# Three bias products of an attention item in row groups of their own, and all rounds of a four-layer cross-attention kernel written out

## The reference

```python
# layers 0, 2
q, k, v = rmsnorm(x, norm_w) @ wq, cond @ wk, cond @ wv     # 16 query heads, 4 key heads
out = x + (softmax(q k^T / sqrt(8)) v) @ wo
# layers 1, 3
col_bias = jnp.zeros((HW, T))                               # 128 tokens x 77 keys
col_bias = col_bias.at[:, token_indices_A].set((-SUPPRESS * (1.0 - mask_A))[:, None])
col_bias = col_bias.at[:, token_indices_B].set((-SUPPRESS * (1.0 - mask_B))[:, None])
logits = einsum('bhqd,bhkd->bhqk', q, k) * scale + col_bias
out = (softmax(logits) v) @ Wo + bo + x
```

## Time and profile before

| | |
|---|---|
| median of 3 runs | 1966.53 us |
| profiled execution | 1973.73 us, its span 1971.9 us |
| TensorE busy | 1882.1 us (95%) |
| VectorE, GpSimd, ScalarE busy | 1677.6 (85%), 1496.9 (76%), 1453.1 us (74%) |
| DMA, transposes and loads | 88.1% share of the 16 engines |
| bias products (L1266) | 384, three per MHA item of 128 |
| mean granted clock of TensorE | 0.969 |

### The profile page before, as it was taken

How to read it: one execution, slowest core, us unless ns; L and a number is a source line. 1 busy time by engine, 2 the same in 40 slices (tenths; PEclk the granted TensorE clock), 3 DMA queues, 4 the chain that set the end, 5 groups by cost and what they waited for, 6 DMA issues and landing times.

```text
span 1971.9 us, 76204 instructions
## 1 busy us (share of the span) xinstructions
PE 1882.1 (95%) x28656; PEld 1578.3 (80%) x28784; DVE 1677.6 (85%) x3516; ACT 1453.1 (74%) x2603; POOL 1496.9 (76%) x1830
## 2 busy tenths in 40 slices
PE   5599999999999999999999999999999999999996
PEld 5478888888788887888788887888878888888884
DVE  7588888898788987888888988889878898888883
ACT  4377777777777776777777777777767777777772
POOL 2478888788787877788777887878878888888872
PEclk7599999999999999999999999999999999999997
DMA  5279999999899998899979997999989999999985
GB/s 160 50 126 167 162 168 167 169 160 163 155 174 167 159 168 150 168 162 161 168 150 169 159 166 145 175 169 160 165 150 176 163 163 163 159 152 170 160 158 107
DMA packets 1164823, 310.79 MB, mean 158 GB/s; under 512 B 1139254, under 2 KB 1163132, under 8 KB 1164412
## 3 DMA queue, kind: packets, MB, share of 16 engines
q1 hardware_dynamic: 1164412, 305.43, 88.1%
HBM read 15.93 MB, written 4.19 MB: 10 GB/s over the span
## 4 chain that ended last, share of the span: by engine, by line
PE 81%; DMA 5%; issue 3%; DVE 3%; SPq 3%; POOL 2%; ACT 2%; ACTq 0%; DVEq 0%
PE ring L1135 46%; PE sc L1268 9%; PE o_ps L1135 8%; DMA arena<-p_sm 5%; PE o_ps L1286 4%; PE ring L1337 4%; PE sc L1251 3%; PE sc L1266 2%; POOL arena L589 1%; PE ring L1206 1%; POOL p_sm L566 1%; ACT arena L627 1%; PE ring L1318 1%; PE ring L1334 1%; PE sc L1243 1%
## 5 line engine op out<-in xcount | busy, mean ns | idle before, releaser
L561 POOL TENSOR_TENSOR p_sg<-arena,p_sg 128x512 f16<-128x512 f32 (+1 forms) x256 | 347.4, 1357 | 216.1 <-ACT p_sg L627 216.1
L1135 PE MATMUL ring<-ctx_two,m_w 128*128 128x154 f16 x6144 | 447.1, 233 | 0.0
L1135 PEld LDWEIGHTS ring<-ctx_two,m_w 128*128 128x128 f16 x6144 | 433.7, 99 | 1.0 <-DVE o_tg L821 0.9
L1004 DVE TENSOR_TENSOR arena<-sc,row_max 128x616 f32<-128x616 f32 (+2 forms) x512 | 405.2, 792 | 4.5
L566 POOL TENSOR_TENSOR p_sm<-arena,p_sm 128x616 f16<-128x616 f32 x256 | 336.8, 1316 | 46.9 <-ACT p_sm L627 46.9
L1135 PE MATMUL ring<-wv_m,ctx_two 128*77 128x512 f16 x1536 | 365.5, 383 | 0.1
L627 ACT ACTIVATE arena<-ring 128x462 f16<-128x462 f32 (+1 forms) x384 | 196.3, 512 | 136.9 <-PE ring L1135 136.9
L589 POOL TENSOR_TENSOR arena<-arena 128x1024 f16<-128x1024 f32 x128 | 273.1, 2133 | 30.2 <-ACT arena L627 19.1
L1135 PEld LDWEIGHTS ring<-wv_m,ctx_two 128*77 128x77 f16 x1536 | 166.0, 117 | 149.9 <-DVE q_mix L825 46.1
L1001 DVE TENSOR_REDUCE row_max<-sc 128x6 f32<-128x462 f32 (+2 forms) x384 | 223.7, 582 | 55.6 <-PE sc L1268 55.5
L1268 PE MATMUL sc<-arena,x_s 128*128 128x512 f16 (+1 forms) x1152 | 262.5, 337 | 7.0
(11 more groups left out here) (160 smaller groups left out, 3529.9 us busy)
## 6 DMA issues: line engine op xcount, KB each, us to landing
ctx_nat<-in_ctx_dram SPq DMA_DIRECT2D x64, 77.0 KB
x_nat<-in_x_dram SPq DMA_DIRECT2D x64, 64.0 KB, 2.2
arena<-p_sg SPq DMA_TRANSPOSE x256, 4.2
arena<-p_sm SPq DMA_TRANSPOSE x256, 3.9
out_dram<-y_out SPq DMA_DIRECT2D x64, 64.0 KB, 2.0
arena<-in_L_xattn_Wk_dram SPq DMA_DIRECT2D x2, 1024.0 KB, 6.0
arena<-in_L_xattn_Wv_dram SPq DMA_DIRECT2D x2, 1024.0 KB, 6.7
arena<-arena SPq DMA_TRANSPOSE x128, 5.8
```

The costliest lines, as they stand in the source:

```text
L561: pool.tensor_tensor(p_sg[k][:, LO, 0:e - a], probs_flat[:, a:e], p_sg[k][:, HI, 0:e - a], ALU.subtract).then_inc(sems["pg_lo"], 1)
L1004: dve.tensor_tensor(shifted[:, hs, :], s_view[:, hs, :], row_max[:, hs].unsqueeze(2).to_broadcast([P, hs.stop - hs.start, S]), ALU.subtrac ...
L1135: ins = pe.matmul(out, a, b, start=(n == 0), stop=(n == len(passes) - 1))
```

## The change

All three bias products of an MHA item are issued together, ahead of the scores of chunk 0. Each takes its six rows from another group of 32 partitions: the product of bank b reads partitions 32b to 32b + 5 of `bias_l` and `bias_r`. For that the prologue copies the six rows to partitions 32 and 64, six more steps of VectorE. Since all three banks are opened at chunk 0, `scores_free` waits there for both halves of the shift, and no longer at chunks 1 and 2. And the loops over the rounds are gone on all five engines: rounds 1 to 7 are written out.

```diff
--- before.py
+++ after.py
@@ -487,11 +487,9 @@
 
             for n in range(-3, PAIRS):
                 pair(0, n)
-            with sp.Fori(1, NIT - 2) as it:
+            for it in range(1, NIT):
                 for n in range(PAIRS):
                     pair(it, n)
-            for n in range(2 * PAIRS):
-                pair(NIT - 2 + n // PAIRS, n % PAIRS)
             for n in range(TAIL):
                 pair(NIT, n)
             for st in range(STREAMS):
@@ -612,11 +610,9 @@
 
             for n in range(-3, PAIRS):
                 pair(0, n)
-            with pool.Fori(1, NIT - 1) as it:
+            for it in range(1, NIT):
                 for n in range(PAIRS):
                     pair(it, n)
-            for n in range(PAIRS):
-                pair(NIT - 1, n)
             for n in range(TAIL):
                 pair(NIT, n)
 
@@ -805,11 +801,9 @@
 
             for n in range(-3, PAIRS):
                 pair(0, n)
-            with act.Fori(1, NIT - 1) as it:
+            for it in range(1, NIT):
                 for n in range(PAIRS):
                     pair(it, n)
-            for n in range(PAIRS):
-                pair(NIT - 1, n)
             for n in range(TAIL):
                 pair(NIT, n)
 
@@ -919,6 +913,10 @@
                 step(dve.tensor_scalar(m[5], mask_p[:, 0, :], row_sel[:, 0:1], None, ALU.mult))
                 step(dve.scalar_tensor_tensor(out=m[6], in0=mask_p[:, 1, :], scalar=row_sel[:, 1:2], in1=m[5], op0=ALU.mult, op1=ALU.add))
                 step(dve.scalar_tensor_tensor(out=bias_l[0:6, :], in0=mask_p[:, 2, :], scalar=row_sel[:, 2:3], in1=m[6], op0=ALU.mult, op1=ALU.add))
+                for k in range(1, 3):
+                    step(dve.tensor_copy(bias_l[32 * k:32 * k + 6, :], bias_l[0:6, :]))
+                    for n in range(2):
+                        step(dve.tensor_copy(bias_r[n][32 * k:32 * k + 6, :, :], bias_r[n][0:6, :, :]))
 
             def split_gqa_weights():
 
@@ -1117,11 +1115,9 @@
 
             for n in range(-3, PAIRS):
                 pair(0, n)
-            with dve.Fori(1, NIT - 1) as it:
+            for it in range(1, NIT):
                 for n in range(PAIRS):
                     pair(it, n)
-            for n in range(PAIRS):
-                pair(NIT - 1, n)
             for n in range(TAIL):
                 pair(NIT, n)
 
@@ -1260,10 +1256,14 @@
                 lead = leader(m)
                 g = g_s[lead // 4 % 2][:, :, stream(m) % 2].rearrange("p a h s -> p a (h s)")
                 pe.wait_ge(sems["g_lo"], at("g_lo", it, lead, G_NEEDED[k]))
-                scores_free(it, m, min(k, 1) + 1)
-                ind = bias_r[w][:, :, :].rearrange("p h s -> p (h s)")
                 a, e = k * BANK, min(HS, (k + 1) * BANK)
-                pe.matmul(sc_flat[:, a:e], bias_l[:, :], ind[:, a:e], start=True, stop=False)
+                if k == 0:
+
+                    scores_free(it, m, 2)
+                    ind = bias_r[w][:, :, :].rearrange("p h s -> p (h s)")
+                    for b in range(3):
+                        c0, c1, rows = b * BANK, min(HS, (b + 1) * BANK), slice(32 * b, 32 * b + 6)
+                        pe.matmul(sc_flat[:, c0:c1], bias_l[rows, :], ind[rows, c0:c1], start=True, stop=False)
                 for x, y in ((HI, HI), (HI, LO), (LO, HI)):
                     ins = pe.matmul(sc_flat[:, a:e], x_s[st][:, x, :], g[:, y, a:e], start=False, stop=(x == LO))
                 ins.then_inc(sems["sm_raw"], 1)
@@ -1375,11 +1375,9 @@
 
             for n in range(-3, PAIRS):
                 pair(0, n)
-            with pe.Fori(1, NIT - 1) as it:
+            for it in range(1, NIT):
                 for n in range(PAIRS):
                     pair(it, n)
-            for n in range(PAIRS):
-                pair(NIT - 1, n)
             for n in range(TAIL):
                 pair(NIT, n)
 
@@ -1387,7 +1385,7 @@
 CONSTS = 19
 ARENA = 15180
 SMALL_LOADS = 20
-DVE_STEPS = 73
+DVE_STEPS = 79
 
 
 # ---- launch: one core; inputs and output as the reference has them ----
```

## The result

| | before | changed |
|---|---|---|
| median | 1965.45 us (4 runs) | 1952.12 us (4 runs, 1951.14 to 1953.31) |
| ratio | | 0.9932, 95% interval 0.9915 to 0.9949 |
| profiled execution, span | 1973.73, 1971.9 us | 1952.95, 1951.2 us |
| short pair, long pair | 13.93, 14.44 to 14.58 us | 14.18, 14.44 us |
| TensorE busy | 1882.1 us | 1871.1 us |

The kernel is 13 us faster, 0.7%. The forecast was 25 us (1941 us, in a range of 1926 to 1976). The two halves of the change pull in opposite directions, as the experiments will show: written-out rounds give about 30 us, grouped bias products take 16 back.

What follows compares the result with a forecast made beforehand. TensorE was taken as the main bound (81% of the chain). Loops -28.1, prologue +3.0, short pairs +12.0 and long pairs -12.3 sum to -25.4: 1948.3 us from the profiled execution, 1941 after the 7.2 to the median; range 1926 to 1976.

Steps and rivals of the forecast that it cites:

- Loops written out: At the jumps between the six loop rounds: writing them out removes the jumps and what follows them, -28.1 us.
- the aftermath: Behind each jump: pipeline refilled by VectorE, GpSimd and the transposes, counted within the 28.1 us.
- Prologue: Ahead of the rounds: six more VectorE steps, all on the path, +3.0 us (2.0 to 3.7).
- The group of three: Ahead of chunk 0's scores: three bias products run side by side in 0.24 us, or 0.52 if one waits for another.
- one after another: Rival, at the group: the three bias products run serially, 0.52 us, 36 us more, 1977 us; 5%.
- The wait at chunk 0: First bias load: 0.38 us late behind the second shift in short pairs, none in long; short pairs net +12.0 us.
- Chunk 2's 0.09 us lost to q_mix: Behind `values_m`: the 0.09 us saved at chunk 2 turns into a longer TensorE wait for q_mix.
- Going into and out of row groups: Around each item's bias group: changing from all rows to 32 and back costs 0, at the other end +50 us.
- the 30% rival: Around the bias products: the mode change empties the array, 0.16 or 0.26 us each, 192 times, 1972 or 1991 us; 30%.
- No new wait: Rival, at chunk 0: VectorE keeps up, 0.28 us an item is kept, -36 us, 1905 us; 4%.
- The jumps aren't the cost: Rival, at the loops: straight code stalls as often, only prologue and bias count, 1969 us; 6%.
- Transposes become the bound: Rival, in pairs that get shorter: transposes bound them, long pairs stay as they are, +12, 1953 us; 7%.

Runs made afterwards that it cites:

- e1: Changed kernel with the bias products of before, each ahead of its own chunk over all rows, without the prologue copies: 1935.79 us, 0.9843 of before.
- e6: Changed kernel, but all three grouped bias products take the same rows 0 to 5, without the prologue copies: 1986.02 us, 1.0098 of before.
- e7: e1 with each bias product, in its own place, restricted to rows 0 to 5: 2001.29 us, 1.0172 of before.
- e2: Kernel before, loops kept, with the three grouped bias products and the six prologue steps: 1983.42 us, 1.0077 of before.
- e10: e1 without the bias product of chunk 2: 1935.56 us, 0.9836 of before.
- e9: e7 with each bias product over rows 0 to 37, a group of 64 rows: 2002.99 us, 1.0190 of before.
- e8: Kernel before with its loops, each engine given a hint on its closing branch at the top of the body: 1944.99 us, 0.9884 of before.
- e11: e1 without the bias product of chunk 1: 1915.51 us, 0.9742 of before.
- e3: Changed kernel, but the three grouped bias products each run over all 128 rows, without the prologue copies: 1968.01 us, 1.0003 of before.

## Why the prediction came out as it did

**Loops written out: right, slightly too small.** -28.1 forecast; e1 gives -30.5 by the medians. A loop also held up pairs away from the jump, which my reference, the first loop round, contained. What the forecast called the aftermath, a pipeline refilled by VectorE, GpSimd and the transposes, is for the most part something else: TensorE at half its clock, about 12.7 of the 28.1 us. The size came from the windows and so was right without it.

**Prologue: right.** +3.0 against 2.5.

**The group of three: right.** The forecast had 0.24 us for the group and 36 us more if the products ran one after another. e6 against the changed kernel is 34 us, and 36 with the copies of the prologue, which e6 doesn't have. A group takes 0.32 us up to the first score, as long as the single product of e7: nothing is lost among the three. The rival "one after another" is out.

**The wait at chunk 0: right in place, kind, pairs and size.** Apart from three of the 67 waits only short pairs have it. Counted from the pair's start the load moved from 5.17 (e1) to 5.55 us, 0.37 us; 0.38 was forecast. Two small differences cancel here, which is luck: the load comes 0.11 us behind the shift instead of 0.05, but the shift itself ends 0.07 us earlier in the pair. In e2 the distance is 0.05 in the looped rounds, where a register instruction takes the other waits and sg_sub alone stands on the product, and 0.11 to 0.12 in its written-out rounds; their short pairs last 14.09 and 14.18 us. A short pair grew by 0.25 us instead of 0.19 because of the way out of the row group: the first score comes 0.46 us later than in e1, where 0.38 + 0.02 was due.

**Chunk 2's 0.09 us lost to q_mix: right**, shown by e10. The waits for q_mix are 53.9 us in the changed kernel against 43.1 in e1, 0.09 each.

**Going into and out of row groups: this is the step that failed.** The forecast took 0, from "the nearest row", and named what it didn't show. There the products change from one half of the partitions to the other, at the same height. Measured are about 0.10 us on the way in and 0.08 to 0.10 on the way out. Both signs that it gave for an array that empties are there: a gap ahead of the first score product in all 128 items (28.6 us in all), and a later first bias product in long pairs. In a long pair both are exposed: 0.18 us, against a saving of 0.19, so that it stayed at 14.44 where about 14.26 was due. 64 long pairs make 11.5 us; in short pairs the way in lies in the wait and the rest adds some 0.06, 4 us. The bias half is thus +18 by the pairs and +16 by the medians instead of +2.7. Its size in the rival's own unit is e = 0.09, below both of its priced points, 0.16 and 0.26, and below 0.132, where it would have outweighed the loops. The mechanism of the 30% rival is real, its price was too high and mine too low. The forecast had put the array's emptying at the whole 0.16 us by which a product's record exceeds its step; the runs show 0.10.

The terms add up: 25.4 us forecast, 2.4 more from the loops, 0.5 from the prologue, 11.9 less from long pairs and 3.9 less from short ones make 12.5; 13.3 were measured. That the time lies in the range is no proof of the forecast's own case: the range had room for a small e, and the forecast's own case had it at 0.

The rule of the Trainium skill, page "TensorEngine Tiling (Array Packing)", section Tiling Modes, Key Properties, that changing the mode drains TensorE while changing the tile doesn't, agrees with these runs: e7 and e9 show a delay at each change, for heights of 32 and 64 rows, of about 0.2 us for in and out together, while the three groups of one height cost nothing among themselves.

**Rivals.** "No new wait" is out (67 waits). "The jumps aren't the cost" is out (e1, e8). "Transposes become the bound" did not decide here, as no pair got shorter than 13.93; e11 shows that it would have been next.

The profiled execution of before lay 7 us above its median, that of the changed kernel 0.8. The forecast took the difference off the sum, so that its change, not its level, came from the trace; comparing the two profiled executions alone would overstate the gain (20.8 us).

## What to carry to other kernels

Small products in row groups do run side by side for the time of one, but each change between whole-height products and a row group keeps the next weight load from running ahead, here about 0.2 us in and out; three products of 0.52 us together (e3) became 0.42 with both ways, and a single one lost 0.2 (e7). Pulling work forward on a busy engine pulls its waits forward too: compare, pair by pair, when the released buffer comes free with when the engine arrives, and ask at each saving which wait stands behind it (0.09 us ahead of q_mix was worth nothing, 0.216 us ahead of `values_m` all of it, until transposes came next). Test the halves of a change alone: here one half hid that the other lost. And look at the granted clock behind every place where TensorE stands still for microseconds: here it doubled the price of the stop.

## What was not expected of the hardware

A jump back over a round of 16 pairs stopped TensorE for 2.6 to 2.9 us and VectorE for up to 5, and cost about 6 us with its aftermath (30.5 us over five). Behind each stop TensorE's granted clock was 0.50 for a while, 27.31 us in all over five jumps, which costs nearly as much as the stops themselves (about 12.7 us against 14.1). A hint given at the top of the body, some 230 us ahead of the jump, removed most of it: 21 to 23 us, at no cost that the runs show.
